# Inputs of an LSTM over image rows: f16 pairs through TensorE, or f32 copied into PSUM by ScalarE

## The chip, the cores and the metric

One core of a Trainium2 chip runs the kernel. The metric is the time of one execution on the device in microseconds; the kernel before took 701.72 us (median of 3 runs, 700.06 to 704.18).

## What is computed

`x` is 32 images of 128 channels and 32x32 pixels, f32. Two residual steps follow each other:

```
x = x + lstm(gn(x))            # L0
x = x + hetconv(gn(x)) + bias  # L1

def lstm(v):                   # one time step per image row, 1024 columns (32 images x 32 pixels)
    xs = conv1x3(v, w_i2s * mask) + b_i2s     # taps left and centre
    h = c = 0
    for r in range(32):
        z = xs[row r] + conv1x3(h, w_s2s) + b_s2s
        i, f, g, o = split(z @ w_ih.T + b_ih + b_hh)
        c = sigmoid(f) * c + sigmoid(i) * tanh(g)
        h = sigmoid(o) * tanh(c)
        out[row r] = h
```

`gn` is a group norm over 32 groups (channels g*4 to g*4+3), each image on its own. `hetconv` is a 3x3 convolution in which each output channel has a full 3x3 kernel for a quarter of the input channels and a centre tap for the others.

## The kernel before, in words

Everything stays in SBUF: `img` holds the 32 images, 128 channels on the partitions. There are three stages, and each engine runs its own list of instructions in program order, with semaphores between them. SyncE's queue issues the loads, four per image.

**First stage, input convolution, about the first 137 us.** Per image b: VectorE takes the statistics (`image_stats`, L413, two instructions), and per chunk of `CH` = 4 images the chain of small steps that ends in scale and bias (`bn_aggr` L420, `chain_mean`, `chain_var`, `chain_rstd`, L425 to L454, with two tiny matmuls L940 and L944 on TensorE and a square root L803 on ScalarE). ScalarE writes the normalised image in f32 (`xn0`, L814). Its f16 high half `hi0` is made by GpSimd for even images (L724) and by ScalarE for odd ones (L821), its low half `lo0` always by GpSimd (L726). TensorE does 12 matmuls per image (L972, L973): two PSUM banks, two taps, three products of high and low halves. Then the result, `xs`, goes back into `img` as a pair of f16 numbers per pixel: high half by ScalarE (L826), low half by VectorE (L552), each in two instructions. `xn0`, `hi0`, `lo0` have two slots, and the banks two sets. In between, the weights are prepared: `scale_weights` (L492 to L514), `split_weights`, `last_weights` on VectorE, transposes on TensorE (L948, L957, L959, L962), `turn` and `wall_hi` on ScalarE (L796, L849).

**Second stage, the LSTM, to about 480 us.** A row is cut into three blocks of 11, 10 and 11 images (352, 320 and 352 columns), so there are 96 items, called `it` here. The items of an engine's list run in order; loops of the hardware (`Fori`) hold two rows each. For one item:

- TensorE: `close_conv` (3 matmuls, L1035 to L1038, on h of the row before, next block), then `open_conv` of item it+1 (L1013: two matmuls that add the two f16 halves of `xs` into the z bank through the scaled identity `spread`; then 6 on h, L1022 and L1025), then `z @ w_ih.T` for the four gates, 12 matmuls (L1055 to L1069), in the order F, I, G, O.
- ScalarE: the four gates in that order (L872), `z_hi` of item it+1 (L861), `tc` = tanh(c) (L879).
- VectorE: `ig` = i*g (L610), the new cell (L614), `z_lo` of item it+1 (L595), `hrow` = o*tanh(c) (L619), its f16 halves `hh` (L622) and `hl` (L624, which reads `hrow` and `hh`), the 32x32 transposes `hT` (L629).
- GpSimd: `forget`, `fc` = f*c (L736), then `place`, which adds `hT` and the rows of x into `img` (L744).

`close_conv` of an item needs `hh` and `hl` of the item two before it.

**Third stage, the 3x3 convolution, to the end.** Statistics, normalisation, four shifted copies by DMA and GpSimd, 39 matmuls per half image (L1098, L1108), residual and stores. The change leaves its work as it is.

The lines that set the order of the LSTM's items on ScalarE and VectorE:

```
act: wait gate_ready -> gate F, I, G, O ; z_hi(it+1) ; wait c_done -> tc(it)
dve: ig(it) ; cell(it) ; z_lo(it+1) ; wait tc_done -> hrow(it) ; hh(it) ; hl(it) ; hT(it)
pool: wait c_done, gate F done -> fc(it+1) ; wait ht_done -> place(it)
```

Of the kernel before, what the change touches and what calls it, by code (L numbers as in the profile page):

```python
# [15 lines left out]
P = 128  # L16
# [12 lines left out]
XS_SCALE = 2.0 ** -14  # L29
# [11 lines left out]
CHUNKS = B // CH  # L41
GN_STEPS = 11
# [4 lines left out]
STATS_AHEAD = 7  # L47
# [28 lines left out]
def build_network(nc, x, w_i2s, b_i2s, w_s2s, b_s2s, w_ih, b_ih, b_hh, w_conv, b_conv, consts, out):  # L76
# [4 lines left out]
    with ExitStack() as ctx:  # L81
# [20 lines left out]
        bn = sb("bn", [P, CH, 2, 6], F32)  # L102
# [7 lines left out]
        bias_top = sb("bias_top", [P, 1], F32)  # L110
# [8 lines left out]
        with ExitStack() as s01:  # L119
# [13 lines left out]
            spread = sb("spread", [P, P], F16, s01)  # L133
            raw_cb = sb("raw_cb", [P, P], F32, s01)
            mask = sb("mask", [P, P], F32, s01)
            with ExitStack() as s0:
                xn0 = [sb(f"xn0{i}", [P, HW], F32, s0) for i in range(2)]
                hi0 = [sb(f"hi0{i}", [P, HW], F16, s0) for i in range(2)]
                lo0 = [sb(f"lo0{i}", [P, HW], F16, s0) for i in range(2)]
                raw_i = sb("raw_i", [P, P, 3], F32, s0)  # L140
                raw_s = sb("raw_s", [P, P, 3], F32, s0)
                raw_g = sb("raw_g", [P, GATES, P], F32, s0)
                raw_c = sb("raw_c", [P, P, 9], F32, s0)
                turn_i = sb("turn_i", [P, 2, P], F32, s0)
                turn_c = sb("turn_c", [P, 9, P], F32, s0)
            with ExitStack() as s1:
# [8 lines left out]
                hh = [sb(f"hh{i}", [P, B * W + 2], F16, s1) for i in range(2)]  # L155
                hl = [sb(f"hl{i}", [P, B * W + 2], F16, s1) for i in range(2)]
# [17 lines left out]
        spread_done = sem("spread_done")  # L174
        raws_ready = sem("raws_ready")
        bias_ready = sem("bias_ready")
        bias_col_zero = sem("bias_col_zero")
# [20 lines left out]
        xs_hi_done = sem("xs_hi_done")  # L198
        xs_lo_done = sem("xs_lo_done")
# [41 lines left out]

        def padded(t, part, half, dh):
# [20 lines left out]
        def xs_part(b, s, part):  # L263
            return img[:, b, H // 2 * s:H // 2 * (s + 1), part, :]
# [9 lines left out]

        def wgroup(n):
            return ps[:, 4 + n, 0:[2, 3, 4][n] * P].rearrange("p (a b) -> p a b", b=P)

        bias_T = ps[:, 4, 3 * P:4 * P]
        bias_ps = bias_T[96:97].rearrange("p (q n) -> p q n", q=Q)
        gate_bias_ps = ps[:, 5, 3 * P:3 * P + GATES]  # L280
# [3 lines left out]

        wconv_ps = ps[:, 4:7, 0:3 * P].rearrange("p d (e o) -> p d e o", o=P)
# [12 lines left out]
        def _(sp):  # L298
            def images(q, b, n):
                return img32[32 * q:32 * q + 32, b:b + n].rearrange("p b h w -> p b (h w)")  # L300

            def load_x(b):
# [4 lines left out]
                for q in QUARTERS:  # L307
                    sp.dma_start(images(q, b, 1), x_q[q, :, b:b + 1, :]).then_inc(x_in[b % (2 * CH)], 16)

            for b in range(STATS_AHEAD):  # L310
                load_x(b)
                if b == 0:
                    sp.dma_start(group_mean[:], consts[1]).then_inc(group_in, 16)
# [77 lines left out]
        def _(v):  # L391
# [784 lines left out]
```

## Time and profile before

| what | value |
|---|---|
| median of 3 runs | 701.72 us |
| the profiled execution | 697.59 us |
| its span, first to last instruction | 695.8 us |
| mean granted clock of TensorE | 0.978 |
| busy: TensorE / VectorE / ScalarE / GpSimd | 90% / 80% / 63% / 61% |
| HBM read, written | 35.07 MB, 16.78 MB |
| chain of waits, by engine | PE 67%, SPq 12%, DVE 8%, DMA 4% |

Times are in microseconds from the start of the span. PE is TensorE, PEld its weight loads, DVE VectorE, ACT ScalarE, POOL GpSimd. L12 is line 12 of the kernel. "Idle before, releaser" is the time in which an engine stood still before an instruction and what ended it. Matmuls overlap, so the distance between the starts of two of them says what one costs, not the duration that is printed.

### The profile page before, as it was taken

How to read it: one execution, taken by the hardware profiler on the slowest of the kernel's cores; microseconds unless marked ns; L12 is line 12 of the kernel's file. 1: busy time of each engine (PE TensorE's matmuls, PEld its weight loads, DVE VectorE, ACT ScalarE, POOL GpSimd, SP SyncE). 2: the span in 40 equal slices, each digit the busy share in tenths (PEclk: the TensorE clock that was granted, in tenths of full speed). 3: DMA queues.
4: the chain of work that ended last, by engine and by line, in shares of the span. 5: the costliest groups of instructions: out<-in, count | busy, mean ns of one | idle time of the engine just before them, and what ended most of it. 6: DMA issues, size and time to landing. Idle time of an engine off the chain costs nothing.

```text
span 695.8 us, 15711 instructions
## 1 busy us (share of the span) xinstructions
PE 627.8 (90%) x5152; PEld 391.4 (56%) x5152; DVE 559.1 (80%) x1236; ACT 441.4 (63%) x779; POOL 421.4 (61%) x386
## 2 busy tenths in 40 slices
PE   1677889899999999999999999993699999999996
PEld 0233434378888888888888888883233333333332
DVE  5798998489999999999999999998576676677442
ACT  1594888777777777777777777774544343334420
POOL 0584777655555555555555555556857677776761
PEclk9998999999999999999999999998599999999999
DMA  9999900004412444314444124400969999999996
GB/s 238 238 279 266 154 4 9 0 1 61 61 25 35 60 60 60 47 19 55 60 60 60 30 30 60 60 0 1 246 201 275 270 271 279 267 274 269 259 272 193
DMA packets 96397, 88.95 MB, mean 128 GB/s; under 512 B 78241, under 2 KB 79521, under 8 KB 96289
## 3 DMA queue, kind: packets, MB, share of 16 engines
q1 hardware_dynamic: 89632, 70.26, 44.7%
q10 hardware_dynamic: 6720, 18.11, 9.2%
q8 instruction: 27, 0.44, 0.3%
q14 instruction: 18, 0.14, 0.1%
HBM read 35.07 MB, written 16.78 MB: 75 GB/s over the span
## 4 chain that ended last, share of the span: by engine, by line
PE 67%; SPq 12%; DVE 8%; DMA 4%; POOL 2%; issue 2%; ACT 2%; ACTq 0%; POOLq 0%; DVEq 0%
PE ps L1108 11%; PE ps L1022 8%; SPq L346 5%; PE ps L1055 5%; PE ps L1059 5%; PE ps L1056 4%; PE ps L1069 4%; PE ps L1067 4%; PE ps L1068 4%; SPq L352 4%; PE ps L1025 4%; PE ps L1013 4%; DMA shifted<-pad 3%; PE ps L1098 3%; PE ps L972 3%; PE ps L973 3%
## 5 line engine op out<-in xcount | busy, mean ns | idle before, releaser
L736 POOL TENSOR_TENSOR fc<-gate,cell 128x352 f32<-128x352 f32 (+1 forms) x96 | 107.6, 1120 | 153.4 <-ACT gate L872 153.4
L872 ACT ACTIVATE gate<-ps,gate_bias 128x352 f32<-128x352 f32 (+1 forms) x288 | 146.7, 549 | 47.5 <-PE ps L1059 30.6
L771 POOL COPY shifted<-pad 32x1073 f32<-32x1073 f32 x128 | 137.5, 1074 | 54.7 <-DVE pad L651 48.4
L1108 PE MATMUL ps<-shifted,wt_hi 128*32 128x512 f16 x1536 | 108.9, 390 | 7.9 <-DMA shifted<-pad 7.8
L658 DVE SCALAR_TENSOR_TENSOR img<-ps,y_unscale,img 128x512 f32<-128x512 f32 x64 | 47.8, 748 | 69.1 <-PE ps L1108 69.1
L893 ACT ACTIVATE pad<-img,nbias,rstd 128x1024 f16<-128x1024 f32 x32 | 39.8, 1244 | 80.7 <-PE ps L1108 72.1
L744 POOL TENSOR_TENSOR img<-hT,xr 128x352 f32 (+3 forms) x96 | 87.2, 908 | 2.7 <-DVE hT L629 2.6
L413 DVE BATCH_NORM_STATS2 bn<-img 128x6 f32<-128x512 f32 x120 | 76.4, 682 | 9.8 <-DMA img<-in_x_dram 9.8
L726 POOL TENSOR_TENSOR lo<-xn,hi 128x1024 f16<-128x1024 f32 x32 | 68.1, 2131 | 18.2 <-PE ps L973 9.2
L1055 PE MATMUL ps<-z_hi,wg_hi 128*128 128x352 f32 (+1 forms) x192 | 70.8, 371 | 2.3 <-ACT z_hi L861 2.2
L1108 PEld LDWEIGHTS ps<-shifted,wt_hi 128*32 128x32 f16 x1536 | 35.2, 96 | 63.6 <-issue 23.4
L879 ACT ACTIVATE tc<-cell 128x352 f32<-128x352 f32 (+1 forms) x96 | 47.0, 490 | 27.5 <-DVE cell L614 27.5
L1067 PE MATMUL ps<-z_hi,wg_hi 128*128 128x352 f32 (+1 forms) x192 | 61.0, 318 | 0.0
L1069 PE MATMUL ps<-z_lo,wg_hi 128*128 128x352 f32 (+1 forms) x192 | 61.0, 318 | 0.0
L1068 PE MATMUL ps<-z_hi,wg_lo 128*128 128x352 f32 (+1 forms) x192 | 60.9, 317 | 0.0
L1056 PE MATMUL ps<-z_hi,wg_lo 128*128 128x352 f32 (+1 forms) x192 | 60.5, 319 | 0.0
L1098 PE MATMUL ps<-pad,wc_hi 128*128 128x512 f16 x128 | 51.0, 400 | 5.7 <-DVE pad L651 5.7
L619 DVE TENSOR_TENSOR hrow<-gate,tc 128x352 f32<-128x352 f32 (+1 forms) x96 | 49.4, 515 | 7.7 <-ACT tc L879 0.6
L610 DVE TENSOR_TENSOR ps<-ps,gate 128x352 f32<-128x352 f32 (+1 forms) x96 | 49.1, 512 | 7.8 <-ACT gate L872 7.6
L595 DVE SCALAR_TENSOR_TENSOR z_lo<-ps,z_unscale,z_hi 128x352 fp32r<-128x352 f32 (+1 forms) x96 | 54.2, 564 | 1.2 <-ACT z_hi L861 1.2
L1108 PE MATMUL ps<-shifted,wt_lo 128*32 128x512 f16 x768 | 54.3, 389 | 0.0
L861 ACT ACTIVATE z_hi<-ps,z_unscale 128x352 fp32r<-128x352 f32 (+1 forms) x96 | 54.0, 563 | 0.0
(139 smaller groups left out, 1437.0 us busy)
## 6 DMA issues: line engine op xcount, KB each, us to landing
shifted<-pad SPq DMA_DIRECT2D x128, 134.1 KB, 4.0
shifted<-pad ACTq DMA_DIRECT2D x128, 134.1 KB, 4.1
img<-in_x_dram SPq DMA_DIRECT2D x128, 128.0 KB, 3.5
xr<-in_x_dram SPq DMA_DIRECT2D x64, 256.0 KB, 5.7
out_dram<-img SPq DMA_DIRECT2D x60, 256.0 KB, 4.5
shifted<-shifted SPq DMA_DIRECT2D x2, 553.5 KB, 5.8
out_dram<-img SPq DMA_DIRECT2D x16, 64.0 KB, 1.8
raw_c<-in_L_conv_W_dram SPq DMA_DIRECT2D x4, 144.0 KB, 2.9
```

The costliest lines, as they stand in the source:

```text
L413: v.bn_stats(bn[:, j, s, :], src[:, 512 * s:512 * s + 512]).then_inc(bn_done, 1)
L736: pool.tensor_tensor(fc[s % 2][:, 0:n], gate[s % 2][0][:, 0:n], cell[:, W * b0:W * b1], ALU.mult).then_inc(fc_done, 1)
L744: pool.tensor_tensor(img32[:, b0:b1, 2 * j + s // NB, :], hT[s % 2][:, 0:width(s % NB)].rearrange("p (b w) -> p b w", w=W), xr[:, slot, b0 ...
L771: pool.tensor_copy(shifted[b % SLOTS][32:64, q, ROWS_AT:ROWS_END].bitcast(F32), pad[b % SLOTS][32 * q:32 * q + 32, ROWS_AT:ROWS_END].bitca ...
L872: act.activation(gbank(s, m)[:, 0:n] if m == 1 else gate[p][m][:, 0:n], gbank(s, m)[:, 0:n], ACT.Tanh if gt == G_GATE else ACT.Sigmoid, bi ...
L1055: pe.matmul(gbank(s, m)[:, 0:n], wg_hi[:, GATE_ORDER[m], :], z_hi[:, 0:n], start=True, stop=False)
L1056: pe.matmul(gbank(s, m)[:, 0:n], wg_lo[:, GATE_ORDER[m], :], z_hi[:, 0:n], start=False, stop=False)
L1067: pe.matmul(gbank(s, m)[:, 0:n], wg_hi[:, GATE_ORDER[m], :], z_hi[:, 0:n], start=True, stop=False)
L1068: pe.matmul(gbank(s, m)[:, 0:n], wg_lo[:, GATE_ORDER[m], :], z_hi[:, 0:n], start=False, stop=False)
L1069: pe.matmul(gbank(s, m)[:, 0:n], wg_hi[:, GATE_ORDER[m], :], z_lo[:, 0:n], start=False, stop=True).then_inc(gate_ready, 1)
L1098: pe.matmul(y_bank(b, s).rearrange("p (h w) -> p h w", w=W), w[:], padded(pad[b % SLOTS], part, s, 0), start=(m == 0), stop=False, skip_gr ...
L1108: ins = pe.matmul(bank[32 * q:32 * q + 32], w[:, d, q, :], padded(shifted[b % SLOTS][:, q], part, s, d - 1), start=False, stop=(m == 2 and ...
```

## The change

- The result of the input convolution is stored as one f32 number per pixel into `img`, by one instruction per image: ScalarE for even images, VectorE for odd ones (`store_xs`).
- In the LSTM, ScalarE copies the f32 inputs of an item into its z bank (`load_xs`), three items ahead; TensorE's two `spread` matmuls go, and its matmuls on h add onto that.
- `hh` is made by GpSimd (`high_h`), ahead of `forget` and `place`; on VectorE `hT` now stands ahead of `hl`.
- First stage: three slots and three sets of banks; chunks of the statistics of 1, 2, 3, 4, 4, 4, 4, 4, 4, 2 images; `hi0` by GpSimd for every fourth image, by ScalarE for the others; 14 images are loaded before the gate and convolution weights, and half of image 0 is issued by ScalarE's queue; the steps for the weights are cut into smaller pieces and spread over more images, the sum of the biases goes to GpSimd, and two instructions of VectorE that read two small SBUF tiles are replaced by others; the memsets of `hh`, `hl`, `cell` shrink or go to GpSimd.

```diff
+FIRST_COUNTS = (1, 2, 3, 4, 4, 4, 4, 4, 4, 2)
+CHAIN_AT = {0: 1, 1: 2, 4: 3, 7: 4, 11: 5, 15: 6, 19: 7, 23: 8, 27: 9}
+STATS_BY = (6, 7, 8, 10, 11, 12, 14) + tuple(range(15, B + 1)) + (B,) * 7
+CONV_SLOTS = 3
+LOADED_FIRST = 14
...
 # vector, first stage
-            def low_xs(b):
-                for s in range(2):
-                    v.wait_ge(xs_hi_done, 2 * b + s + 1)
-                    v.scalar_tensor_tensor(out=xs_part(b, s, 1), in0=rows(y_bank(b, s)), scalar=XS_SCALE,
-                                           in1=xs_part(b, s, 0), op0=ALU.mult, op1=ALU.subtract).then_inc(xs_lo_done, 1)
+            def store_xs(b):
+                v.wait_ge(xconv_done, b + 1)
+                v.tensor_copy(image(b), flat(x_banks(b))).then_inc(xs_odd_done, 1)
...
             for b in range(B):
+                g = CHAIN_AT.get(b)
+                if b >= EVAC_LAG and b % 2:
+                    store_xs(b - EVAC_LAG)
+                if g is not None:
                     chain_mean(g)
+                for i in range(STATS_BY[b - 1] if b else STATS_FIRST, STATS_BY[b]):
+                    image_stats(i)
+                if g is not None:
                     chain_var(g)
                     chain_rstd(g, g % 2)
+                if b + 1 in CHAIN_AT:
+                    bn_aggr(CHAIN_AT[b + 1])
...
 # vector, LSTM item
                 v.tensor_tensor(hrow[u][:, cols], gate[p][3][:, 0:n], tc[p][:, 0:n], ALU.mult).then_inc(h_done, 1)
                 v.wait_ge(h_done, H_AHEAD + it + 1)
+                v.wait_ge(row_done, it + 1)
+                v.transpose(hT[p][:, 0:n], hrow[u][:, cols]).then_inc(ht_done, 1)
                 if not final_step:
-                    v.tensor_scalar(hh[u][:, pads], hrow[u][:, cols], ACT_SCALE, None, ALU.mult).then_inc(hh_done, 1)
                     v.wait_ge(hh_done, NB + it + 1)
                     v.scalar_tensor_tensor(out=hl[u][:, pads], in0=hrow[u][:, cols], scalar=ACT_SCALE,
                                            in1=hh[u][:, pads], op0=ALU.mult, op1=ALU.subtract).then_inc(hl_done, 1)
-                v.wait_ge(row_done, it + 1)
-                v.transpose(hT[p][:, 0:n], hrow[u][:, cols]).then_inc(ht_done, 1)
...
 # gpsimd
+            def high_h(j, s):
+                u = s // NB
+                b0, b1 = BLOCKS[s % NB]
+                pool.wait_ge(h_done, H_AHEAD + 2 * NB * j + s + 1)
+                pool.sem_inc(waited, 1)
+                pool.tensor_scalar(hh[u][:, 1 + W * b0:1 + W * b1], hrow[u][:, W * b0:W * b1], ACT_SCALE, None,
+                                   ALU.mult).then_inc(hh_done, 1)
...
                     for s in range(2 * NB):
+                        high_h(2 * i + slot, s)
                         forget(2 * i + slot + (s + 1) // (2 * NB), (s + 1) % (2 * NB))
                         place(2 * i + slot, s, slot, i + 1)
...
 # scalar
+            def load_xs(it, s, t):
+                n = width(s % NB)
+                b0, b1 = BLOCKS[s % NB]
+                act.wait_ge(z_lo_done, Z_AHEAD + it - 1)
+                act.activation(zbank(s)[:, 0:n].rearrange("p (b w) -> p b w", w=W), img32[:, b0:b1, t, :],
+                               ACT.Copy).then_inc(xs_loaded, 1)
...
                 act.activation(tc[p][:, 0:n], cell[:, W * b0:W * b1], ACT.Tanh).then_inc(tc_done, 1)
+                if loads:
+                    load_xs(it + 3, s + 3, 2 * j + (s + 3) // NB)
...
 # tensor
-                for half in range(2):
-                    ins = pe.matmul(z.rearrange("p (b w) -> p b w", w=W), spread[:], img[:, b0:b1, t, half, :],
-                                    start=(half == 0), stop=row0 and half == 1)
...
-                    pe.wait_ge(z_lo_done, it + 1)
-                    open_conv(2 * j + (s + 1) // NB, s + 1, (k + 1) % NB, zero_state and s + 1 < NB)
+                if not last and not (zero_state and s + 1 < NB):
+                    pe.wait_ge(xs_loaded, it + 2)
+                    open_conv(2 * j + (s + 1) // NB, s + 1, (k + 1) % NB)
```

## Rows read from the trace of the kernel before

**Rows 1.** Stages: start:end, length, busy time (x instructions) of each engine, clock, DMA share, GB/s.
```profile
40.00:60.00 20.00, 13.27 (x54) 5.61 (x53) 18.28 (x50) 12.00 (x16) 12.55 (x7) 0.87 1.00 276
110.00:140.00 30.00, 26.96 (x127) 12.35 (x126) 17.70 (x41) 25.43 (x38) 22.30 (x14) 1.00 0.03 3
300.00:400.00 100.00, 100.00 (x654) 80.60 (x652) 93.34 (x199) 78.62 (x171) 57.26 (x58) 1.00 0.33 47
```

**Rows 2.** Timeline of TensorE, first stage: start, length, instruction, idle before and releaser.
```profile
23.95 0.59 PE L972 MATMUL ps<-hi,wi_hi 128*128 128x512 f16 x1 [5.33 <-POOL hi L724]
...
31.62 0.38 PE L972 MATMUL ps<-hi,wi_hi 128*128 128x512 f16 x1
...
55.88 0.59 PE L972 MATMUL ps<-hi,wi_hi 128*128 128x512 f16 x1 [6.07 <-DVE img L552]
...
135.07 0.38 PE L973 MATMUL ps<-lo,wi_hi 128*128 128x496 f16 x1
```

**Rows 3.** Groups of first-stage instructions by shape, 85 to 145 us: busy, mean ns.
```profile
L726 POOL TENSOR_TENSOR lo<-xn,hi 128x1024 f16<-128x1024 f32 x16 | 34.1, 2130 | 6.8 <-PE ps L973 3.4 <-ACT hi L821 2.8
L552 DVE SCALAR_TENSOR_TENSOR img<-ps,img 128x512 f16<-128x512 f32 x35 | 22.3, 679 | 8.1 <-ACT img L826 8.1
L814 ACT ACTIVATE xn<-img,nbias,rstd 128x1024 f32<-128x1024 f32 x15 | 18.6, 1241 | 1.1 <-POOL lo L726 0.5
L826 ACT ACTIVATE img<-ps 128x512 f16<-128x512 f32 x34 | 18.2, 586 | 4.1 <-PE ps L973 4.1
...
L821 ACT ACTIVATE hi<-xn 128x1024 f16<-128x1024 f32 x8 | 8.4, 1056 | 0.0
L724 POOL CAST hi<-xn 128x1024 f16<-128x1024 f32 x7 | 7.2, 1035 | 1.4 <-PE ps L973 1.4
```

**Rows 4.** Timeline of VectorE, first stage and the first LSTM items.
```profile
7.69 1.29 DVE L413 BATCH_NORM_STATS2 bn<-img 128x6 f32<-128x512 f32 x2 [4.65 <-DMA img<-in_x_dram]
...
51.00 0.83 DVE L501 TENSOR_TENSOR bsum<-brow 128x1 f32<-128x1 f32 x1
...
52.20 1.93 DVE L507 SCALAR_TENSOR_TENSOR top<-bias_top,top 128x1 f32<-128x1 f32 x1
...
141.74 0.54 DVE L595 SCALAR_TENSOR_TENSOR z_lo<-ps,z_unscale,z_hi 128x320 fp32r<-128x320 f32 x1
142.38 0.53 DVE L619 TENSOR_TENSOR hrow<-gate,tc 128x352 f32<-128x352 f32 x1
...
143.33 0.53 DVE L624 SCALAR_TENSOR_TENSOR hl<-hrow,hh 128x352 f16<-128x352 f32 x1
```

**Rows 5.** Timeline of GpSimd, the same stretches.
```profile
49.69 2.12 POOL L726 TENSOR_TENSOR lo<-xn,hi 128x1024 f16<-128x1024 f32 x1
51.99 2.12 POOL L726 TENSOR_TENSOR lo<-xn,hi 128x1024 f16<-128x1024 f32 x1 [0.18 <-ACT hi L821]
...
139.95 0.93 POOL L736 TENSOR_TENSOR fc<-gate,cell 128x352 f32<-128x352 f32 x1 [5.90 <-ACT gate L872]
143.39 1.19 POOL L736 TENSOR_TENSOR fc<-gate,cell 128x320 f32<-128x320 f32 x1 [2.51 <-ACT gate L872]
```

**Rows 6.** Timeline of ScalarE: first normalised image, F gates of items 0 to 3, z_hi.
```profile
21.47 2.37 ACT L814 ACTIVATE xn<-img,nbias,rstd 128x1024 f32<-128x1024 f32 x2 [1.94 <-DVE nbias L454]
...
139.25 0.56 ACT L872 ACTIVATE gate<-ps,gate_bias 128x352 f32<-128x352 f32 x1 [1.16 <-PE ps L1059]
...
141.01 0.55 ACT L861 ACTIVATE z_hi<-ps,z_unscale 128x320 fp32r<-128x320 f32 x1
...
142.78 0.53 ACT L872 ACTIVATE gate<-ps,gate_bias 128x320 f32<-128x320 f32 x1 [0.43 <-PE ps L1059]
...
149.83 0.55 ACT L872 ACTIVATE gate<-ps,gate_bias 128x352 f32<-128x352 f32 x1 [0.48 <-PE ps L1059]
```

**Rows 7.** Timeline of TensorE, gates of item 1.
```profile
141.61 0.41 PE L1055 MATMUL ps<-z_hi,wg_hi 128*128 128x320 f32 x1 [0.96 <-ACT z_hi L861]
```

**Rows 8.** Group of tanh(c) by shape, 110 to 500 us.
```profile
L879 ACT ACTIVATE tc<-cell 128x352 f32<-128x352 f32 x64 | 31.9, 499 | 19.6 <-DVE cell L614 19.6
```

More of the change, by code:

```diff
@@ L1 @@
+import itertools
 import struct
@@ L261, in y_bank, with x_banks, xs_stored @@
             return ps[:, 2 * (b % 2) + s, :]
-        def xs_part(b, s, part):
-            return img[:, b, H // 2 * s:H // 2 * (s + 1), part, :]
+        def x_banks(b):
+            first = 2 * ((b + 1) % CONV_SLOTS)
+            return ps[:, first:first + 2, :]
+        def xs_stored(engine, b):
+            return engine.wait_ge(xs_odd_done if b % 2 else xs_even_done, b // 2 + 1)
         def rows(t):
@@ L949, in turn, with turn_conv @@
                 ins.then_inc(prep_T, 1)
[L951 removed]
+            def turn_conv(d):
                 pe.wait_ge(raws_ready, 3)
[L954 to L963 removed]
@@ L965, in input_conv @@
-            def input_conv(b):
-                pe.wait_ge(hi0_done, b + 1)
-                def taps(s, w, t, first, last):
-                    bank = rows(y_bank(b, s))
-                    pixels = rows(t[:])[:, H // 2 * s:H // 2 * (s + 1)]
-                    pe.matmul(bank, w[:, 1, :], pixels, start=first, stop=False)
-                    return pe.matmul(bank[:, :, 1:W], w[:, 0, :], pixels[:, :, 0:W - 1], start=False, stop=last)
-                for s in range(2):
-                    if b >= 2:
-                        pe.wait_ge(xs_lo_done, 2 * (b - 2) + s + 1)
-                    taps(s, wi_hi, hi0[b % 2], True, False)
-                    taps(s, wi_lo, hi0[b % 2], False, False)
+                pe.wait_ge(split_done, 3 + d)
@@ new lines, in turn_conv @@
+                for e in range(3):
+                    ins = pe.transpose(wconv_ps[:, e, :], turn_c[:, 3 * d + e, :], ident[:])
+                if d == 0:
+                    pe.wait_ge(bias_summed, 2)
+                    pe.wait_ge(wgt_done, 1)
+                    for k in range(GATES):
+                        ins = pe.matmul(gate_bias_ps[:, k:k + 1], wgT[:, k, :], bsum[:, 0:1], start=True, stop=True)
+                if d == 2:
+                    pe.wait_ge(bias_ready, 1)
+                    ins = pe.transpose(bias_T, bias_col[:], ident[:])
@@ new lines, in turn_conv, with taps, input_high @@
+                ins.then_inc(prep_T, 1)
+            def taps(b, s, w, t, first, last):
+                bank = rows(x_banks(b)[:, s, :])
+                pixels = rows(t[:])[:, H // 2 * s:H // 2 * (s + 1)]
+                pe.matmul(bank, w[:, 1, :], pixels, start=first, stop=False)
+                return pe.matmul(bank[:, :, 1:W], w[:, 0, :], pixels[:, :, 0:W - 1], start=False, stop=last)
+            def input_high(b, s):
+                pe.wait_ge(hi0_done, b + 1)
+                if b >= CONV_SLOTS:
+                    xs_stored(pe, b - CONV_SLOTS)
+                taps(b, s, wi_hi, hi0[b % CONV_SLOTS], True, False)
+                taps(b, s, wi_lo, hi0[b % CONV_SLOTS], False, False)
```

401 lines of the change are left out of this document (217 added, 184 removed).

## The prediction

> **What bounds the kernel now.** I read the stages first. In the LSTM TensorE is busy without a gap and VectorE 93% of the time [rows 1]: 654 matmuls in 100 us are 28.4 items of 23 matmuls, so an item takes 3.52 us and a matmul 0.153 us. That looks like a bound by matmuls. The start of the stage says otherwise. Item 0 and item 1 issue 14 matmuls each (no `close_conv`, only two in `open_conv`) and item 2 issues 20, 48 in place of 69. Still the F gates of items 0, 1 and 3 start at 139.25, 142.78 and 149.83 [rows 6]: 3.53 us for the first item, 10.58 us for three, which is 3.53 each. TensorE even stood idle for 0.96 us before the gates of item 1 [rows 7], and no time came of it. What holds is a loop through ScalarE and VectorE: four gates at 0.44 us each, F at 139.25 to `z_hi` at 141.01 [rows 6]; G is done at 139.25 + 0.88 + 0.55 = 140.68, then `ig`, the cell, `z_lo` from 141.74 to 142.28 [rows 4], and F of item 1 follows 0.50 us later [rows 6]. The branch over `z_hi` (done at 141.56, TensorE at 141.61 [rows 7], four matmuls, the low one) arrives at the same time. So the reader is to see two bounds that lie within a few hundredths of each other: TensorE at 3.52, the loop at about 3.5.
>
> In the first stage nothing is full over its whole length. Image 0 comes in at 7.69 us [rows 4], but the first normalisation starts at 21.47 [rows 6] and the first matmul at 23.95 [rows 2], since a chunk is four images. From the fourth image's matmuls (31.62) to the end of the last (135.07 + 0.38 = 135.45) are 103.8 us for 29 images, 3.58 each [rows 2], where 12 matmuls cost 12 x 26.96/127 = 2.55 us [rows 1]. The rest is waiting: 6.07 us before 55.88, for VectorE [rows 2], at a time in which two of its instructions on single columns took 0.83 and 1.93 us [rows 4]. GpSimd then ran two `lo0` [rows 5], from 49.69 to 51.81 and 51.99 to 54.11, and the two VectorE instructions end at 51.83 and 54.13: both read two tiles in SBUF, and both stood until GpSimd's was over.
>
> **First stage, the start.** The first chunk has one image: statistics 1.29 us from about 7 [rows 4], two tiny matmuls and the chain with the scale of the weights in between, some 5 us by estimate (2 to 8; it does not enter the sum), so normalisation at about 13 and, with image 1 and 2's statistics ahead of the chunk's matmul on TensorE, first matmuls at about 17. Then chunk 1 waits behind the statistics of images 3 to 5 (3 x 1.29), its square root and matmuls at the lower of TensorE's two levels, 1.2 GHz, that is at twice 0.212 us: the trace has such matmuls behind idle time at 23.95 and 55.88, printed with 0.59 where 0.38 is usual, in a stage whose granted clock is 0.87 [rows 1, 2]. I place the fourth image at about 32 us, where it was. The early start is spent; I count 0.
>
> **First stage, the rate.** Per image, after: TensorE 2.55. ScalarE 1.24 (normalise) + 3/4 x 1.06 (`hi0`) + 1/2 x 1.17 (store: two halves of 586 ns in one) = 2.62, less 0.11 per neighbour that overlaps (two normalisations took 2.37, not 2.48 [rows 3, 6]), so 2.3, and some 6 us once for weights. Before it was 1.24 + 0.53 + 1.17 = 2.94. GpSimd 2.13 + 1/4 x 1.04 = 2.39, before 2.65 [rows 3], which was the rate of undisturbed pairs. VectorE 1.29 + 1/2 x 1.36 = 1.97, before 2.65, plus chains. The store is not shown in the trace: it lies between 0.68 (one of today's halves) and 1.36 us (both); I take 1.2, the end nearer to equal elements, and it is off the bound either way. So TensorE becomes the bound: 29 x 2.55 = 74 us, some 5 us for transposes and tiny matmuls, and 4 us of waits for chains: 83 us. **Gain 103.8 - 83 = about 21; I take 20**, between 13 (5 to 7 us more of waits) and 24. The stalls on two-tile instructions go with the new forms. The loads stay ahead: an image is 4 x 128 KB, 1.9 us at 276 GB/s [rows 1], and one is used every 2.6 or more.
>
> **Hand-over.** Last matmul's end to F of item 0: 139.25 - 135.45 = 3.80 us. After: one store of image 31 on VectorE (1.2), `z_lo` (0.54), 0.50 to F, 2.3; the table load and the first `load_xs` lie before it. Gain 1.5.
>
> **LSTM, two matmuls less per item.** 2 x 0.153 x 96 = 29 us of TensorE's time. By the loop above, which does not pass through them, I count 1 us (3.52 to 3.51), with 5 as the end on that side.
>
> **`load_xs` on ScalarE.** Not in the trace; nearest is `tc`, 499 ns for 352 columns [rows 8]. It waits for `z_lo` of the next item, and F of that item stands behind it. In item 0: `z_lo` done 142.28, load to about 142.28 + 0.03 + 0.50 - 0.11 = 142.70, F started at 142.78 [rows 4, 6]. It fits with 0.08 us to spare: price 0, and if the overlap fails 0.03, or 0.1 with a slow strided read: 0 to 10 us.
>
> **`hh` on GpSimd.** VectorE loses 0.34 us per item that no loop used. On GpSimd its price is not in the trace: from below 1035 x 352/1024 = 356 ns by the cast of `hi0` [rows 3], from above 927 ns, the multiply `fc` of the same width undisturbed [rows 5]. A one-input instruction is nearest to the cast; with a fixed part I take 0.45. GpSimd is 57% busy and has room: `hrow` is done at 142.91 [rows 4], `hh` runs to 143.4, and `fc` of item 1, which could start at 143.31 + 0.07, is 0.05 late; it is needed when `ig` is done, at about 144.7, and ends at 144.3. `hl` moves from 143.33 to 143.45 behind `hT`. `close_conv` of item 2 then has it in time, TensorE having 0.3 us more room per item. Price 0, up to 8 us in all.
>
> The rest of the change, with the third stage, is 0: nothing there is altered.
>
> **Sum** against the profiled execution: 697.6 - 20 - 1.5 - 1 = 675.1. The median of the runs is 4.1 above that execution, so 701.7 - 22.5 = **679 us**. Its own range is 667 (24 and 5 gained, a little less elsewhere) to 692.
>
> **Rival 1, slower: `hl` is held by `fc`.** The rows just read show that a VectorE instruction on two SBUF tiles stands until a running GpSimd instruction is over. The reverse is there too: `fc` began at 143.39, 0.06 after `hl`, and took 1.19 us where it takes 0.93 alone [rows 4, 5]. Today `hl` always comes first. After the change `hh` and `fc` follow each other on GpSimd without a gap, and `hl` can only begin when `hh` is done: F of item 1 ends at 143.31, `hh` at 143.4, so `fc` starts with or before `hl`. Then `hl` stands for 0.93 us, to 144.8 instead of 143.95, and `ig` of item 1, due at 142.78 + 0.88 + 0.55 = 144.2, is 0.5 late, and with it the loop. It decides from the point at which `hh` ends later than F of the next item. In blocks where that happens: 32 x 0.5 = 16 us for each of the three blocks of a row, so 695, 711 or 727; I take 711 as the case. For it: the times above. Against it: 0.1 us in either direction, GpSimd's start-up against VectorE's shorter one, decides each item. The Trainium skill (SBUF — State Buffer, the practical consequences on shared ports) states this as a rule that speaks against the change: of a VectorE instruction with two SBUF inputs and a GpSimd instruction that reads SBUF, the second to issue blocks fully until the first is done. By that rule the trace agrees, 0.83 us for a single column; by it the kernel ends at 695 or above. Chance 0.25, a third of it at 695.
>
> **Rival 2: TensorE was the bound.** Then an item takes 21 x 0.153 = 3.21 us, 29 us less: 701.7 - 21.5 - 29 = 651. For it: 100% busy [rows 1]. Against: items 0 to 2. Chance 0.07.
>
> **Rival 3: the first stage runs into the next wait.** ScalarE's square roots and scales come from chains that wait for TensorE and VectorE in turn; at 2.9 us per image instead of 2.55, 29 x 0.35 = 10 us come back: 690. Chance 0.10.
>
> **Forecast** as summed: 0.58. The range of 8 in 10 runs from 666 to 704: it leaves out rival 2 (0.07) and the upper two outcomes of rival 1 in most of their spread (0.13). Within 0.5% of before (3.5 us, about what a measurement of this kernel can tell) lie only part of rival 1 and a worse rival 3: 0.05. Slower 0.15, faster 0.80.
>
> **What would show it.** Right: fourth image's matmuls near 32 us, the last near 116, F of item 0 near 118; TensorE in the LSTM some 91% busy, still at 3.5 us per item; `hh` on GpSimd near 0.45 us, `hl` 0.53; `load_xs` near 0.5 with F straight behind it. Wrong: `hl` of 1 us and more with an idle ScalarE (rival 1); 3.2 us per item (rival 2); gaps on TensorE in the first stage after the fourth image (rival 3).

## The result, and the profile after

The changed kernel takes 782.3 us (median of 4 runs, 781.2 to 786.1), against 700.9 us (696.9 to 704.2) for the kernel before in the same series: 1.117 times as long, 95% interval 1.110 to 1.125. The forecast was 679 us with a range of 666 to 704. The profiled execution spans 781.1 us (before 695.8) at a granted clock of 0.977 (before 0.978). Of all executions told of below, one, of the version in experiment 7, lay more than 1.5% above the fastest of its own kernel, and it is left out of the median and the ratio given there.

Three parts of the page of the kernel after: busy time of each engine, the chain of waits by engine, and groups (busy, mean ns of one, idle time before them and its releaser).

```profile
PE 641.6 (82%) x4968; PEld 366.9 (47%) x4968; DVE 576.6 (74%) x1111; ACT 480.8 (62%) x838; POOL 514.3 (66%) x478
...
DVE 28%; PE 17%; POOL 16%; issue 14%; SPq 11%; ACT 7%; DMA 4%; POOLq 2%; ACTq 1%; DVEq 0%
...
L778 POOL TENSOR_SCALAR hh<-hrow 128x352 f16<-128x352 f32 (+1 forms) x93 | 99.1, 1066 | 138.6 <-DVE hrow L643 138.6
...
L650 DVE SCALAR_TENSOR_TENSOR hl<-hrow,hh 128x352 f16<-128x352 f32 (+1 forms) x93 | 112.4, 1209 | 68.1 <-POOL hh L778 68.1
...
L770 POOL TENSOR_TENSOR fc<-gate,cell 128x352 f32<-128x352 f32 (+1 forms) x96 | 87.0, 906 | 8.0 <-ACT gate L939 8.0
...
L1122 PE MATMUL ps<-hl,ws_hi 128*128 128x352 f16 (+1 forms) x93 | 29.2, 314 | 49.7 <-DVE hl L650 49.7
```

TensorE was 67% of the chain before and is 17% now; VectorE and GpSimd took its place. `hh` takes 1.07 us on GpSimd, and `hl` behind it 1.21 us on VectorE where it took 0.53 [rows 4].

Two stretches of the kernel after, one in the first stage and one in the LSTM, in the columns of [rows 1]:

```profile
40.00:60.00 20.00, 19.45 (x96) 9.20 (x95) 18.39 (x53) 18.83 (x20) 18.14 (x11) 1.00 0.88 251
...
300.00:400.00 100.00, 80.22 (x462) 56.47 (x461) 81.75 (x132) 72.06 (x154) 67.32 (x67) 1.00 0.23 32
```

In the LSTM an item now has 21 matmuls, and 462 of them are 22.0 items in 100 us, 4.55 us each, against 3.52 before. That is 1.03 us for each of 96 items, 99 us. The first stage did get shorter. ScalarE's timeline of the kernel after, at the F gate of item 0:

```profile
124.35 0.47 ACT L927 ACTIVATE ps<-img 128x352 f32<-128x352 f32 x1 [2.21 <-DVE z_lo L619]
124.75 0.56 ACT L939 ACTIVATE gate<-ps,gate_bias 128x352 f32<-128x352 f32 x1
```

It was at 139.25 [rows 6], so 14.5 us earlier. Together 695.8 - 14.5 + 99 = 780.3, of 781.1 measured: both differences are placed, and nearly all of the loss is in the LSTM. One item there, on VectorE, GpSimd and ScalarE in turn:

```profile
300.91 0.53 DVE L643 TENSOR_TENSOR hrow<-gate,tc 128x352 f32<-128x352 f32 x1
301.47 0.55 DVE L647 STREAM_TRANSPOSE hT<-hrow 128x352 f32<-128x352 f32 x1
302.76 1.24 DVE L650 SCALAR_TENSOR_TENSOR hl<-hrow,hh 128x352 f16<-128x352 f32 x1 [0.74 <-POOL hh L778]
303.92 0.52 DVE L634 TENSOR_TENSOR ps<-ps,gate 128x352 f32<-128x352 f32 x1
304.48 0.53 DVE L638 TENSOR_TENSOR cell<-ps,fc 128x352 f32<-128x352 f32 x1
304.97 0.55 DVE L619 SCALAR_TENSOR_TENSOR z_lo<-ps,z_unscale,z_hi 128x320 fp32r<-128x320 f32 x1
305.56 0.53 DVE L643 TENSOR_TENSOR hrow<-gate,tc 128x352 f32<-128x352 f32 x1
```

```profile
301.63 1.09 POOL L778 TENSOR_SCALAR hh<-hrow 128x352 f16<-128x352 f32 x1 [1.57 <-DVE hrow L643]
302.69 0.93 POOL L770 TENSOR_TENSOR fc<-gate,cell 128x352 f32<-128x352 f32 x1
```

```profile
305.03 0.50 ACT L946 ACTIVATE tc<-cell 128x352 f32<-128x352 f32 x1
305.66 0.47 ACT L927 ACTIVATE ps<-img 128x352 f32 x1
306.10 0.53 ACT L939 ACTIVATE gate<-ps,gate_bias 128x320 f32<-128x320 f32 x1
```

Read them by starts: `hrow` 300.91, `hh` 301.63, `hl` 302.76, `ig` (L634) 303.92, the cell 304.48, `tc` 305.03, the next `hrow` 305.56. These steps, 0.72 + 1.13 + 1.16 + 0.56 + 0.55 + 0.53, close a loop of 4.65 us: `ig` stands behind `hl` in VectorE's order, and `hl` behind `hh`. A second branch runs beside it: `fc` also stands behind `hh` and ends at 303.62, and the cell needs it. Here it has 0.8 us to spare, since the cell starts at 304.48 behind `ig`.

### The profile page after: what moved, and what is told of

It reads as the page before. It is cut to its first block, busy times and chain, and to the rows that moved or that the text cites. A ratio compares the mean times of both kernels' runs of the same rounds, so it can differ in the third digit from the quotient of the medians.

```text
span 781.1 us, 15715 instructions
## 1 busy us (share of the span) xinstructions
PE 641.6 (82%) x4968; PEld 366.9 (47%) x4968; DVE 576.6 (74%) x1111; ACT 480.8 (62%) x838; POOL 514.3 (66%) x478
## 4 chain that ended last, share of the span: by engine, by line
DVE 28%; PE 17%; POOL 16%; issue 14%; SPq 11%; ACT 7%; DMA 4%; POOLq 2%; ACTq 1%; DVEq 0%
POOL fc L770 11%; PE ps L1195 9%; SPq L371 7%; DVE cell L638 6%; DVE ps L634 6%; DVE hrow L643 6%; POOL hh L778 4%; ACT tc L946 4%; SPq L377 4%; DMA shifted<-pad 3%; PE ps L1047 3%; PE ps L1048 3%; DVE z_lo L619 2%; PE ps L1185 2%; DVE bn L438 2%
## 5 line engine op out<-in xcount | busy, mean ns | idle before, releaser
L778 POOL TENSOR_SCALAR hh<-hrow 128x352 f16<-128x352 f32 (+1 forms) x93 | 99.1, 1066 | 138.6 <-DVE hrow L643 138.6
L650 DVE SCALAR_TENSOR_TENSOR hl<-hrow,hh 128x352 f16<-128x352 f32 (+1 forms) x93 | 112.4, 1209 | 68.1 <-POOL hh L778 68.1
L786 POOL TENSOR_TENSOR img<-hT,xr 128x352 f32 (+3 forms) x96 | 112.3, 1170 | 2.6 <-DVE hT L647 2.6
L770 POOL TENSOR_TENSOR fc<-gate,cell 128x352 f32<-128x352 f32 (+1 forms) x96 | 87.0, 906 | 8.0 <-ACT gate L939 8.0
L1122 PE MATMUL ps<-hl,ws_hi 128*128 128x352 f16 (+1 forms) x93 | 29.2, 314 | 49.7 <-DVE hl L650 49.7
L1160 PE MATMUL ps<-z_lo,wg_hi 128*128 128x352 f32 (+1 forms) x192 | 61.0, 318 | 0.0
L1147 PE MATMUL ps<-z_lo,wg_hi 128*128 128x352 f32 (+1 forms) x192 | 49.1, 337 | 10.9 <-DVE z_lo L619 10.9
## 6 DMA issues: line engine op xcount, KB each, us to landing
raw_c<-in_L_conv_W_dram SPq DMA_DIRECT2D x4, 144.0 KB, 3.0
```

The costliest lines, as they stand in the source:

```text
L650: v.scalar_tensor_tensor(out=hl[u][:, pads], in0=hrow[u][:, cols], scalar=ACT_SCALE, in1=hh[u][:, pads], op0=ALU.mult, op1=ALU.subtract).t ...
L770: pool.tensor_tensor(fc[s % 2][:, 0:n], gate[s % 2][0][:, 0:n], cell[:, W * b0:W * b1], ALU.mult).then_inc(fc_done, 1)
L778: pool.tensor_scalar(hh[u][:, 1 + W * b0:1 + W * b1], hrow[u][:, W * b0:W * b1], ACT_SCALE, None, ALU.mult).then_inc(hh_done, 1)
L786: pool.tensor_tensor(img32[:, b0:b1, 2 * j + s // NB, :], hT[s % 2][:, 0:width(s % NB)].rearrange("p (b w) -> p b w", w=W), xr[:, slot, b0 ...
```

## The experiments

The first four ask which part of the change costs the time; the next three, what bounds the LSTM with `hh` on VectorE; then the first stage and the price of `hh` itself. Ratios are to the kernel before, run beside them.

**1. The change with `hh` back on VectorE.** The order on VectorE is `hh`, `hl`, `hT`, as before.

```diff
 # vector
+                    v.tensor_scalar(hh[u][:, pads], hrow[u][:, cols], ACT_SCALE, None, ALU.mult).then_inc(hh_done, 1)
...
 # gpsimd
-                        high_h(2 * i + slot, s)
...
```

> The changed kernel with the high half of h made by VectorE again, ahead of hl, as before; everything else as changed. Theory (the whole loss comes from hh on GpSimd: 1.09 us for it, then hl held 0.7 us by fc): an item falls from 4.55 to about 3.5 us, hl back to 0.53 and fc to 1.05 to 1.2 us, total 782 - 99 = 683 us, range 675 to 690. Rival (load_xs, standing ahead of the F gate, costs as well): an item of 3.6 to 3.8 us, total 693 to 712. Rival (TensorE was the bound before): 3.2 us per item, total about 655.

Measured: 686.9 us (686.4 to 688.1), ratio 0.981 (0.978 to 0.984). Its stretch of the LSTM:

```profile
300.00:400.00 100.00, 97.94 (x594) 74.59 (x592) 92.99 (x199) 89.97 (x198) 55.79 (x57) 1.00 0.38 52
```

594/21 = 28.3 items, 3.53 us each, the rate of before. So moving `hh` costs the whole 95 us (782.3 - 686.9), and the rest of the change is worth 14 us. This version beats both kernels. `hT` moved together with `hh`, but in the kernel after VectorE stands idle for 0.74 us between `hT` and `hl`, so the new place of `hT` costs nothing there.

**2. The kernel before, with `hh` alone on GpSimd,** and `hT` ahead of `hl` as in the change.

```diff
 # vector
-                    v.tensor_scalar(hh[u][:, pads], hrow[u][:, cols], ACT_SCALE, None, ALU.mult).then_inc(hh_done, 1)
...
 # gpsimd
+                        high_h(2 * i + slot, s)
...
```

> The kernel before with this one part of the change: hh by GpSimd ahead of fc, hT ahead of hl. Theory: an item goes from 3.52 to 4.5 to 4.6 us, 96 times 1.0, so 701 + 97 = about 798 us, with hh 1.09, hl 1.2 and TensorE idle in every item. Rival (the loss needs load_xs too, through ScalarE): clearly less, 3.6 to 4.2 us per item, 710 to 765 us.

Measured: 796.4 us (793.9 to 801.3), ratio 1.136 (1.132 to 1.140). The move does the same harm where TensorE still makes the inputs: a ratio of 1.136 is 95 us on a kernel of 701. GpSimd and VectorE in it:

```profile
300.43 1.01 POOL L742 TENSOR_SCALAR hh<-hrow 128x320 f16<-128x320 f32 x1 [1.36 <-DVE hrow L619]
301.41 0.93 POOL L734 TENSOR_TENSOR fc<-gate,cell 128x352 f32<-128x352 f32 x1
```

```profile
301.48 1.21 DVE L626 SCALAR_TENSOR_TENSOR hl<-hrow,hh 128x320 f16<-128x320 f32 x1 [0.70 <-POOL hh L742]
```

**3. A short `hh` on GpSimd.** The changed kernel with a plain copy to f16; the factor 512 is left out of `hh`, and `hl`, which is 512 h less `hh`, takes over the rest with fewer digits.

```diff
-                pool.tensor_scalar(hh[u][:, 1 + W * b0:1 + W * b1], hrow[u][:, W * b0:W * b1], ACT_SCALE, None,
-                                   ALU.mult).then_inc(hh_done, 1)
+                pool.tensor_copy(hh[u][:, 1 + W * b0:1 + W * b1], hrow[u][:, W * b0:W * b1]).then_inc(hh_done, 1)
```

> The changed kernel with GpSimd's multiply by 512 and rounding replaced by a plain copy with rounding, which leaves the factor 512 out of hh (hl keeps it). It prices the duration apart from the lock. If the duration of hh is a matter of the operation, it falls from 1.09 to about 0.46 us, an item gets 0.6 us shorter, about 3.9 to 4.0 us, and hl stays at 1.2 us since fc still follows hh at once: that is rival 1 as it was priced (0.5 per item over 3.5). Total about 782 - 58 = 724 us. If a one-input operation with an f16 output costs 1.09 us whatever it is, nothing moves: 782 us. If the lock was no matter of its own, an item falls to 3.5 and the total to about 682.

Measured: 716.2 us (712.1 and 720.3), ratio 1.023 (1.015 to 1.031); 546 matmuls in 300 to 400 us, 26.0 items, 3.85 us each. Now `hh` takes what I had forecast. GpSimd, then VectorE, over two items:

```profile
300.09 0.48 POOL L778 CAST hh<-hrow 128x352 f16<-128x352 f32 x1 [1.54 <-DVE hrow L643]
300.67 1.26 POOL L770 TENSOR_TENSOR fc<-gate,cell 128x352 f32<-128x352 f32 x1
...
303.86 0.48 POOL L778 CAST hh<-hrow 128x352 f16<-128x352 f32 x1 [1.05 <-DVE hrow L643]
304.30 0.86 POOL L770 TENSOR_TENSOR fc<-gate,cell 128x320 f32<-128x320 f32 x1
```

```profile
300.61 0.53 DVE L650 SCALAR_TENSOR_TENSOR hl<-hrow,hh 128x352 f16<-128x352 f32 x1
...
304.38 1.17 DVE L650 SCALAR_TENSOR_TENSOR hl<-hrow,hh 128x352 f16<-128x352 f32 x1
```

Whichever starts second is held until about the end of the first. In the first item `hl` began at 300.61 and `fc` at 300.67: `fc` took 1.26 us instead of 0.93. In the second `fc` began at 304.30 and `hl` at 304.38, and `hl` took 1.17 instead of 0.53; it ended 0.39 us after `fc`. The shorter `hh` is thus worth 4.55 - 3.85 = 0.70 us per item. That includes collisions, for `hl` is held in every item of the changed kernel and in two of three here (56 of the 86 between 150 and 480 us). What is left, 3.85 - 3.53 = 0.32, is nearly all the collision's, as the F gates of ScalarE show:

```profile
300.03 0.56 ACT L938 ACTIVATE gate<-ps,gate_bias 128x352 f32<-128x352 f32 x1
...
303.61 0.51 ACT L938 ACTIVATE gate<-ps,gate_bias 128x320 f32<-128x320 f32 x1
...
307.49 0.55 ACT L938 ACTIVATE gate<-ps,gate_bias 128x352 f32<-128x352 f32 x1
```

From one F gate to the next are 3.58 us where `hl` was free, and 3.88 where it was held. The mean distances from 150 to 470 us, from the F gate of the block named to the next (the `hl` that runs in that time is the one of the item before):

| block | experiment 1, `hl` free in all | here |
|---|---|---|
| first, 352 columns (`hl` free here) | 3.59 us | 3.60 us |
| second, 320 columns (`hl` held here) | 3.45 us | 3.88 us |
| third, 352 columns (`hl` held here) | 3.64 us | 4.10 us |

Only the items with a held `hl` are longer, by 0.43 and 0.46 us, which is 0.30 per item over the three.

**4. `fc` waits for `hl`,** in the changed kernel, so that `hl` is never second.

```diff
             def forget(j, s, behind_low=False):
...
+                if behind_low:
+                    pool.wait_ge(hl_done, NB + it)
```

> The changed kernel with one more wait: fc of the next item starts only when hl is done, so that the two never meet. Theory (hl stands until fc is over, by the shared way into SBUF): hl falls from 1.21 to 0.53 us, right behind hh; fc ends 0.6 us later than now and takes over as what the cell waits for, so an item gets only 0.1 to 0.3 us shorter, 4.25 to 4.45 us, total 755 to 773 us. Rival (hl is slow for another reason, such as its operands): hl stays at 1.2 us and an item gets longer by about 0.9 us, total about 865 us.

Measured: 777.3 us (775.1 and 779.5), ratio 1.110 (1.105 to 1.116), against 1.117 (1.110 to 1.125) of the change. GpSimd and VectorE in it:

```profile
301.62 0.94 POOL L772 TENSOR_TENSOR fc<-gate,cell 128x352 f32<-128x352 f32 x1 [0.65 <-DVE hl L650]
```

```profile
301.01 0.53 DVE L650 SCALAR_TENSOR_TENSOR hl<-hrow,hh 128x352 f16<-128x352 f32 x1 [0.74 <-POOL hh L780]
301.45 0.53 DVE L634 TENSOR_TENSOR ps<-ps,gate 128x352 f32<-128x352 f32 x1
302.66 0.52 DVE L638 TENSOR_TENSOR cell<-ps,fc 128x352 f32<-128x352 f32 x1 [0.68 <-POOL fc L772]
```

`hl` is back at 0.53 us or less in every item, and only some 5 us come of it: the cell now waits 0.68 us for the later `fc`. So an order is no cure for the collision: what `hl` gains, `fc` loses. What the collision alone makes of the 95 us this run can't show. An estimate from starts: with 0.44 us from `hl` to `ig`, as here, in place of 1.16 in the loop of 4.65 us, that item would take about 3.9 us, since `fc` there is in time. No run has a long `hh` with neither a held `hl` nor a later `fc`.

**5. Both of these together:** the plain copy to f16 (with the factor left out as in 3) and `fc` behind `hl`.

> hh on GpSimd as a plain copy to f16 (0.48 us, the factor 512 left out) and fc waiting for hl. If the lock between fc and hl is what hh_as_plain_cast (716 us, 3.85 us per item) still loses beside the 0.48 us, hl takes 0.53 us in every item, the item about 3.65 us (3.55 to 3.75) and the kernel about 697 us (688 to 706). If hl is slow for another reason, it stays near 1.2 us before the 320-column block and the time at 716 us or above it, since fc then only starts later.

Measured: 718.7 us (718.1 to 720.0), ratio 1.026 (1.021 to 1.032), no faster than 716.2. VectorE in it:

```profile
300.77 0.53 DVE L650 SCALAR_TENSOR_TENSOR hl<-hrow,hh 128x352 f16<-128x352 f32 x1
...
302.42 0.53 DVE L638 TENSOR_TENSOR cell<-ps,fc 128x352 f32<-128x352 f32 x1 [0.40 <-POOL fc L772]
```

The expectation of 697 was wrong by 22 us, and instructively: `hl` is never held, and the item stays at 3.85 us (545 matmuls in 100 us). The order costs as much as the collision that it removes. Where in experiment 3 two items of three were longer, here all three are (3.88, 3.85 and 3.89 us between F gates, in the order of the table there), with the cell behind a late `fc`. Held or ordered, `hl` or `fc` is late. Whether another place of `fc` in GpSimd's list would avoid both was not tried.

**6. Was TensorE the bound?** The kernel before with one `spread` matmul an item; the low half of the inputs is left out of the sum.

```diff
-                for half in range(2):
+                for half in range(1):
...
```

> The kernel before with only one of the two matmuls that bring xs into the z bank: the low half of xs is left out of the sum, so TensorE has 22 matmuls per item in place of 23, and nothing else moves. Theory (the loop over ScalarE and VectorE sets 3.52 us per item, and TensorE's full row is a coincidence): no change, 701 us, within 3 us. Rival (TensorE bounds the item): 96 x 0.153 = 15 us less, 686 us.

Measured: 702.5 us (10 runs, 697.5 to 704.2), ratio 1.001 (0.998 to 1.004).

```profile
300.00:400.00 100.00, 100.00 (x626) 77.88 (x625) 93.44 (x200) 79.05 (x171) 56.96 (x57) 1.00 0.31 44
```

22 matmuls an item now, 626/22 = 28.5 items: 3.51 us, where 23 took 3.52. TensorE's row still prints 100 us of 100, with 28 matmuls fewer in it. A full row was no bound.

**7. Is it ScalarE's gates?** The kernel before with the I gate's activation cut to 32 columns; the other columns of I are left as sums.

```diff
-                    act.activation(gbank(s, m)[:, 0:n] if m == 1 else gate[p][m][:, 0:n], gbank(s, m)[:, 0:n],
+                    r = 32 if m == 1 else n
+                    act.activation(gbank(s, m)[:, 0:r] if m == 1 else gate[p][m][:, 0:r], gbank(s, m)[:, 0:r],
```

> The kernel before, with the I gate's activation cut to its first 32 columns (the rest of the gate stays the raw sum): both branches of the loop get 0.24 to 0.27 us shorter, TensorE's work stays. Theory (two bounds at the same height): TensorE's 23 matmuls still take 3.5 us, so little or nothing, 0 to 5 us less, 696 to 701 us. If the loop alone bounded the item and TensorE had room: 96 x 0.25 = 24 us less, 677 us.

Measured: 692.8 us (three executions, 690.6 to 697.6), ratio 0.987 (0.981 to 0.994). So ScalarE is in the loop, but something else stops the gain early. Its stretch, from the profiled execution (the fourth, 701.8 us, at full clock here):

```profile
300.00:400.00 100.00, 100.00 (x662) 83.08 (x662) 93.68 (x202) 74.25 (x174) 53.37 (x58) 1.00 0.37 51
```

662/23 = 28.8 items, 3.47 us each. The starts of TensorE's matmuls follow each other at 0.15 us, 0.28 at the longest, through whole items, and the F gate at 300.91 waited 0.62 us for TensorE, against 0.43 at [rows 6]. This points to TensorE's own 23 matmuls as what holds 3.47 us, some 0.05 below the loop; one trace shows it, and no second experiment.

**8. The same cut in the version of experiment 1,** where TensorE has two matmuls less.

> The changed kernel with hh on VectorE, and the same short I gate. Here TensorE has 21 matmuls, some 3.21 us, and the loop is shorter by 0.24 to 0.27. Theory: now the two matmuls that the change saves are worth something, an item takes 3.25 to 3.35 us instead of 3.53, 687 - 22 = 665 us, range 660 to 670. Rival (load_xs fills ScalarE so that its own seven instructions are the bound): 3.4 us or more, 675 us or more; and if something else holds 3.53 us, 687 us.

Measured: 674.1 us (670.1 to 675.5), ratio 0.958 (0.953 to 0.964); 618/21 = 29.4 items, 3.40 us each, and I had expected 3.25 to 3.35. VectorE in it:

```profile
302.64 0.53 DVE L648 SCALAR_TENSOR_TENSOR hl<-hrow,hh 128x352 f16<-128x352 f32 x1
303.08 0.54 DVE L653 STREAM_TRANSPOSE hT<-hrow 128x352 f32<-128x352 f32 x1
303.54 0.47 DVE L634 TENSOR_TENSOR ps<-ps,gate 128x320 f32<-128x320 f32 x1
```

`ig` follows `hT` without a gap, and VectorE's row is 94.7 us of 100. In this item the starts are `hrow` 301.70, `hh` 302.26, `hl` 302.64, `hT` 303.08, `ig` 303.54, the cell 304.04, `tc` (ScalarE) 304.57 and the next `hrow` 305.07, and ScalarE stood idle for 0.44 us before `tc`. So VectorE's order, with `tc` in it, is now the loop that holds, at 3.4 us. Together with experiments 6 and 7: the loop through ScalarE and VectorE holds 3.53, TensorE's 23 matmuls about 3.47, and VectorE's order 3.40. By this reading, taking `hh` off VectorE could give nothing by itself, and less work on ScalarE alone little.

**9. The first stage: is ScalarE its pace?** Experiment 1's version, with `hi0` by GpSimd for every second image, not every fourth.

```diff
-                if b % 4 == 0:
+                if b % 2 == 0:
```

> The changed kernel with hh on VectorE, and in the first stage GpSimd makes hi0 for every second image again (as before) in place of every fourth. ScalarE then spends 0.26 us less per image (2.47 in place of the 2.73 at which its four-image pattern runs), GpSimd 0.26 more (2.65). Theory (ScalarE paces the first stage after the change at 2.73 us per image): the rate moves to GpSimd's 2.65 to 2.75, so 0 to 2 us less, 685 to 687 us. If ScalarE was not the pace: GpSimd's extra time shows as 3 to 8 us more.

Measured: 688.5 us (686.2 to 692.9), ratio 0.981 (0.975 to 0.987): nothing. From 40 to 60 us ScalarE fell from 18.92 (experiment 1's version) to 17.10 us of 20, and TensorE stayed:

```profile
40.00:60.00 20.00, 19.50 (x96) 9.15 (x95) 18.48 (x51) 17.10 (x18) 19.68 (x12) 1.00 0.84 251
...
80.00:100.00 20.00, 18.13 (x81) 8.72 (x82) 16.00 (x52) 13.81 (x14) 13.20 (x9) 0.83 0.57 70
```

TensorE is near its limit from 40 to 60 us (19.5 us of 20). What is short is the stretch from 80 to 100, with 81 matmuls and a clock of 0.83.

**10. The weights' steps moved.** In the version of experiment 1, the steps for the maximum of the weights come five images earlier, the turning of the weights two later.

```diff
-BIAS_AT, TOP_AT, SCALE_AT, TURN_CONV_AT = 16, (17, 18), 20, 21
+BIAS_AT, TOP_AT, SCALE_AT, TURN_CONV_AT = 16, (12, 13), 20, 23
```

> The changed kernel with hh on VectorE (hh_on_vector, 686.9 us) and, beside it, the three steps that turn the convolution's own weight scales moved away from the image at which they fall now (the stretch 80 to 100 us, where only 81 of 96 matmuls ran and the clock was 0.83). If the 7 us that the first stage lacks lie in that stretch, the windows 80 to 100 hold over 90 matmuls and the time is 681 to 684 us. If the stretch only moves, or if the first stage's pace is set elsewhere, it stays at 687 us (within 2).

Measured: 685.4 us (6 runs, 680.4 to 687.7), ratio 0.977 (0.973 to 0.982). The run's name and the expectation call the steps later or moved away; the maxima in fact come earlier. Its stretch, and the last matmul of the stage:

```profile
80.00:100.00 20.00, 19.64 (x101) 9.65 (x99) 16.73 (x56) 18.20 (x18) 16.45 (x10) 1.00 0.41 50
```

```profile
119.57 0.38 PE L1047 MATMUL ps<-lo,wi_hi 128*128 128x496 f16 x1
```

The hole is gone, 101 matmuls and a full clock, and the stage ends 3.4 us earlier (the same matmul started at 122.96 in experiment 1's version). Of that the medians show 1.5 us, which their intervals don't separate from nothing. It is the fastest version of this study that computes everything.

**11. The price of `hh` with nothing beside it.** Experiment 1's version, with five instructions of 352 columns in GpSimd's idle start.

```diff
+            pool.memset(src[:, 0:352], 1.0).then_inc(bench, 1)
+            pool.wait_ge(bench, 1)
+            pool.tensor_scalar(lo0[0][:, 0:352], src[:, 0:352], ACT_SCALE, None, ALU.mult).then_inc(bench, 1)
+            pool.tensor_scalar(src[:, 352:704], src[:, 0:352], ACT_SCALE, None, ALU.mult).then_inc(bench, 1)
+            pool.tensor_copy(lo0[0][:, 352:704], src[:, 0:352]).then_inc(bench, 1)
+            pool.tensor_copy(src[:, 704:1056], src[:, 0:352]).then_inc(bench, 1)
```

> hh on VectorE, and five GpSimd instructions of 128 x 352 elements in its idle start: fill with zeros, times 512 to f16, times 512 to f32, copy to f16, copy to f32. If the multiplication itself is the dear part, both products take about 1.09 us and both copies about 0.48 us with nothing beside them; if neighbours' traffic in the LSTM made hh slow, the products take near 0.5 us here. The kernel's time stays at 687 us.

Measured: 688.6 us (685.6 and 691.5). GpSimd's timeline:

```profile
2.13 1.09 POOL L739 TENSOR_SCALAR lo<-turn_c 128x352 f16<-128x352 f32 x1
3.19 1.09 POOL L740 TENSOR_SCALAR turn_c<-turn_c 128x352 f32<-128x352 f32 x1
4.23 0.48 POOL L741 CAST lo<-turn_c 128x352 f16<-128x352 f32 x1
4.65 0.48 POOL L742 COPY turn_c<-turn_c 128x352 f32<-128x352 f32 x1
```

VectorE's first instruction comes at 5.37 us, so no VectorE instruction runs beside these. The multiplication costs 1.09 us with an f16 and with an f32 output, and a copy 0.48 us with either. `hh` in the LSTM was not slowed by a neighbour; it is simply that dear.

## Why the prediction was wrong

**The step that failed: "`hh` on GpSimd", a one-input instruction nearest to the cast, 0.45 us, price 0.** It takes 1.09 us. The upper bound, 927 ns by the two-input multiply `fc`, was itself too low: with one input the multiplication by a constant is dearer than `fc` with two. By the difference of the two widths, a column costs (1092 - 1013)/32 = 2.5 ns in the multiplication by a constant (means of the two forms) and (928 - 861)/32 = 2.1 ns in `fc`. With 1.09 us put into my own sum, `hh` would have run from 142.9 to 144.0, and `fc` and `hl` after it: that its bounds, 356 and 927 ns with up to 8 us in all, did not hold this is why the range failed, not only the median.

**The mechanism of rival 1 was right, its price for the forecast duration too, and it was not the whole cause.** With `hh` at 0.48 us the kernel took 716 us, where the rival said 711 with `hl` held in two blocks of three (experiment 3). It was held in two of three, at 0.43 and 0.46 us where the rival had 0.5. That `hl` stands while `fc` runs is shown in single instructions. By the Trainium skill (SBUF — State Buffer, Summary: rules for kernel authors) the second of two such instructions to issue blocks until the first is done; the trace agrees in both orders, 1.17 us for `hl` and 1.26 us for `fc` where they take 0.53 and 0.93 alone. Ordering the two saved 5 us of 95 (experiment 4) and none of the last 30 (experiment 5), because `fc` then came late. The long `hh` and the held `hl` lie one behind the other in the same loop: 1.13 and 1.16 us of its 4.65. So the case "`hh` goes on without a price" was wrong even at 0.45 us: I had followed `hh` to `fc`, and found `fc` 0.05 us late, and `hh` to `hl`, 0.12 late, but each for an item alone and not in the loop `hrow`, `hh`, `hl`, `ig`, cell, `tc`, `hrow`, where VectorE's order makes every lateness of `hl` a lateness of `ig`. This loop was the one to sum: with 1.09 us in it, 4.65 us are read off one item.

**TensorE, rival 2: right against it.** Two matmuls less an item changed 3.52 to 3.53 us (experiment 1), one less 3.52 to 3.51 (experiment 6). I counted 1 us and got none. That VectorE's 0.34 us "that no loop used" were free to move was right only from VectorE's side.

**`load_xs`: right.** It takes 0.47 us (forecast near 0.5), F stands straight behind it, and in experiment 1's version the item keeps its length with it in: price 0.

**First stage: one row was misread, and the size was off.** Normalisation starts at 12.73 us (forecast about 13), and the fourth image's matmuls at 32.04 (forecast about 32). But the prediction took 31.62 of the kernel before for the fourth image. It is the third: 12 matmuls each of images 0 and 1 start at 23.95 and 28.82, and the fourth image's at 35.03. The fourth image, in the kernel before and then in the one after:

```profile
35.03 0.38 PE L972 MATMUL ps<-hi,wi_hi 128*128 128x512 f16 x1 [0.66 <-DVE img L552]
...
32.04 0.38 PE L1047 MATMUL ps<-hi,wi_hi 128*128 128x512 f16 x1
```

So the early start gave 3.0 us where I counted 0. From there to the end of the last matmul were 135.45 - 35.03 = 100.4 us for 29 images, 3.46 each and not 3.58, and are 122.48 - 32.04 = 90.4 now. That is a gain of 10.0 from the rate, where I took 20. TensorE became the bound, as said, with 84.3 us busy of the 90.4. But the term "some 5 us for transposes and tiny matmuls, and 4 us of waits" was too small: 12 matmuls at 0.216 us are 2.59 us, 75 for 29 images. Of the other 15 TensorE stood idle for 6; the rest, some 9, are transposes, tiny matmuls and some matmuls at the lower clock behind the longest wait (their starts from 83.30 to 86.29 us lie 0.43 us apart, at a granted clock of 0.50 from 84 to 86 us). These are two of the three longest waits, TensorE's timeline of the changed kernel:

```profile
78.94 0.39 PE L1016 MATMUL ps<-mv,group_mean 128*128 128x4 f32 x2 [1.20 <-DVE mv L445]
82.07 0.39 PE L1021 MATMUL ps<-vdev,group_mean 128*128 128x4 f32 x2 [1.86 <-DVE vdev L459]
```

VectorE was at the maxima of the convolution's weights then, before the statistics' chain:

```profile
78.92 0.93 DVE L524 TENSOR_REDUCE cand<-raw_c 32x1 f32<-32x288 f32 x2
...
81.86 0.16 DVE L459 TENSOR_TENSOR vdev<-ps,mv 128x4 f32<-128x4 f32 x1
```

Experiment 10 moved these, with the turning of the weights, and took 3.4 us of the stage; the wait before `vdev`'s matmuls fell from 1.9 us to 0.4 at the longest. Which of the two moves did it was not separated. So rival 3, which gave 10 us back, was nearer than the forecast for this stage: 93 us against 83, and 90.4 came.

**Hand-over: right.** 124.75 - 122.48 = 2.27 us, forecast 2.3. With 3.0 and 10.0 it makes the 14.5 us by which the LSTM begins earlier.

Put together, everything but `hh` came to 14 us where I had 22.5, and `hh` with its collision to 95 where I had 0 to 8. The chance of 0.15 for slower was built on the collision alone; a rival "`hh` is dearer than its neighbours in the table" had no place among them, though the duration was called unknown.

## What to carry to other kernels

An operation that the trace does not show on its new engine should not be priced by its number of inputs. Where it lies in a loop that is already the bound, ask what the loop gives at a price above the dearest neighbour's, and let the range hold that. A longer step can also push two others onto each other, and the loop pays for both. Room on an engine (GpSimd was 57% busy) says nothing about a step that others wait for: what counts is the loop from one `hrow` to the next, summed through every engine's order, and it is worth writing down as a chain of starts, as above.

## What was unexpected of the hardware

- GpSimd multiplies 128 x 352 f32 numbers by a constant in 1.09 us, with an f16 or an f32 output, and copies or converts them in 0.48 us (experiment 11). The product of two f32 tiles of that size takes 0.93 us, less than the product with a constant.
- The collision of a VectorE instruction with two inputs in SBUF and a GpSimd instruction works in either order: a start 0.06 to 0.08 us earlier decides which of the two is late (experiment 3). Putting the two in a fixed order cost as much as the collision (716.2 and 718.7 us, experiments 3 and 5).
- A TensorE row of 100 us in 100 stayed so when the number of matmuls in it fell from 654 to 626 (experiment 6): the printed busy time of overlapping matmuls can't tell a full engine from one with 4% less to do.
